# A Mamba block on one core: u = silu(conv + bias) as one Silu pass of ScalarE instead of a tanh form shared by ScalarE and VectorE

## The reference, cut to what matters

```python
xz = jnp.einsum('ed,bld->bel', in_proj_w, hidden_states)
out_f = _mamba_dir(xz, ...)
out_b = _mamba_dir(xz[:, :, ::-1], ...)[:, :, ::-1]

def _mamba_dir(xz, ...):
    x, z = xz[:, :256], xz[:, 256:]
    u = jax.nn.silu(causal_conv(x, conv_w) + conv_b)
    x_dbl = jnp.einsum('bdl,kd->bkl', u, xproj_w)            # 8 + 16 + 16 rows
    delta = softplus(einsum(dtproj_w, x_dbl[:, :8]) + dt_bias)
    dA  = exp(delta * A)                                     # 256 x 512 x 16 states
    dBx = delta * Bm * u
    h = scan(dA, dBx)                                        # along the 512 tokens
    y = einsum(h, Cm) + Dp * u
    return y * silu(z)
```

## Time and profile before

| | |
|---|---|
| device time, median of 3 runs | 922.49 us (917.73 to 923.41) |
| device time of the profiled execution | 920.03 us |
| its span, first to last instruction | 917.9 us |
| DVE busy | 814.2 us, 89% |
| ACT busy | 782.7 us, 85% |
| PE busy, POOL busy | 754.4 us, 749.2 us |
| mean granted TensorE clock | 0.942 |

### The profile page before, as it was taken

How to read it: one execution, slowest core, us unless ns; L and a number is a source line. 1 busy time by engine, 2 the same in 40 slices (tenths; PEclk the granted TensorE clock), 3 DMA queues, 4 the chain that set the end, 5 groups by cost and what they waited for, 6 DMA issues and landing times. The chain is left out here.

```text
span 917.9 us, 13850 instructions
## 1 busy us (share of the span) xinstructions
PE 754.4 (82%) x3873; PEld 377.3 (41%) x3873; DVE 814.2 (89%) x846; ACT 782.7 (85%) x1454; POOL 749.2 (82%) x446
## 2 busy tenths in 40 slices
PE   3477988889887897978898898978989787997975
PEld 1224434353443535334363535435353443634343
DVE  2249889998999989998999989999899989999995
ACT  2488998899979997999979999799979999799850
POOL 2028979889797998889798898979988897988984
PEclk9778999999999999999999999999999999999787
DMA  3242408061350707134080603407071331707000
GB/s 96 71 115 78 98 4 196 3 145 31 86 122 3 171 3 163 45 85 86 28 181 3 157 17 98 108 18 156 3 169 39 92 79 34 163 4 172 0 16 20
DMA packets 51401, 72.52 MB, mean 79 GB/s; under 512 B 6688, under 2 KB 19888, under 8 KB 51376
## 3 DMA queue, kind: packets, MB, share of 16 engines
q1 hardware_dynamic: 50944, 71.95, 33.7%
q10 hardware_dynamic: 432, 0.26, 0.1%
HBM read 60.66 MB, written 11.53 MB: 79 GB/s over the span
## 5 line engine op out<-in xcount | busy, mean ns | idle before, releaser
L693 POOL TENSOR_TENSOR hst<-hst,c_rep 128x1024 f32<-128x1024 f32 x256 | 601.3, 2372 | 113.7 <-DVE hst L580 113.6
L580 DVE TENSOR_TENSOR_SCAN hst<-da,b_ps 128x512 f32<-128x512 f32 x512 | 585.0, 1200 | 31.2 <-PE b_ps L884 12.6
L417 ACT ACTIVATE da<-rep,neg_a 128x511 f32<-128x511 f32 x512 | 337.0, 710 | 27.8 <-DVE hst L580 26.4
L884 PE MATMUL b_ps<-ident,dbx_t 128*128 128x128 f32 x1536 | 240.0, 295 | 104.3 <-DVE hst L580 100.2
L884 PEld LDWEIGHTS b_ps<-ident,dbx_t 128*128 128x128 f32 x1536 | 177.6, 148 | 247.0 <-DVE hst L580 207.3
L406 ACT ACTIVATE dbx_t<-du_t,b_t 128x256 f32<-128x256 f32 x576 | 248.3, 495 | 3.4 <-PE b_ps L884 1.9
L901 PE MATMUL y<-hst,sum_sel 128*32 128x512 f32 x1024 | 149.2, 658 | 12.8 <-POOL hst L693 12.8
L797 PE MATMUL pb<-xnt,conv_wt 128*128 128x512 f32 x256 | 120.9, 617 | 1.4 <-ACT xnt L317 0.8
L869 PE MATMUL b_ps<-t_log,spread_sel 32*128 32x512 f32 x256 | 92.7, 670 | 10.2 <-POOL t_log L749 9.0
L703 POOL TENSOR_TENSOR dbx_t<-du_t,b_t 128x1024 f32<-128x1024 f32 x48 | 91.7, 1909 | 2.7 <-ACT du_t L389 2.7
L568 DVE TENSOR_TENSOR b_ps<-b_ps,b_rep 128x1024 f32<-128x1024 f32 x64 | 77.8, 1216 | 1.6 <-PE b_ps L869 1.6
(11 more groups left out here) (111 smaller groups left out, 608.1 us busy)
## 6 DMA issues: line engine op xcount, KB each, us to landing
rep<-d_scr SPq DMA_DIRECT2D x128, 256.0 KB, 9.1
c_rep<-bc_scr SPq DMA_DIRECT2D x64, 256.0 KB, 5.1
d_scr<-t_pos SPq DMA_DIRECT2D x15, 512.0 KB, 2.9
b_rep<-bc_scr SPq DMA_DIRECT2D x64, 64.0 KB, 2.4
x_ln<-x SPq DMA_DIRECT2D x8, 256.0 KB, 3.5
x_res<-x SPq DMA_DIRECT2D x8, 256.0 KB, 2.9
out<-x_res SPq DMA_DIRECT2D x8, 256.0 KB, 6.0
conv_wt<-conv_w SPq DMA_DIRECT2D x2, 512.0 KB, 6.0
```

Source lines behind the costliest of these rows:

```text
L417: nc.scalar.activation(da[s % 2][:, j, 1:L], rep[d][h][:, j, 1:L], ACT.Exp, scale=neg_a[:, d, h, j, q:q + 1]).then_inc(decay_done, 1)
L580: nc.vector.tensor_tensor_scan(hst[s % RING][:, j, :], da[s % 2][:, j, :], b_ps[:, j, :], 0.0, ALU.mult, ALU.add).then_inc(scan_done, 1)
L693: nc.gpsimd.tensor_tensor(hst[s % RING][:, two, :], hst[s % RING][:, two, :], c_rep[d][:, q:q + 1, :].broadcast_to([P, 2, L]), ALU.mult).t ...
L884: ins = tr(b_ps[:, j, P * c:P * (c + 1)], dbx_t[(NX * d + q - 1) % 2][:, c, NJ * h + j, :, :].rearrange("p r e -> p (r e)"), ident[:, :])
```

## The change

Both ACT passes and the DVE operation on each half of u become one ACTIVATE, Silu with the convolution's bias, from the bank straight into `u[d]`. Both halves stand together in slot 1 of ACT's list, after `inputs_t(d, U, 1, 3)`. At half 0 it takes over DVE's wait for the reader of the old u (`sum_done`) and waits for `du_ready` of the unit before. The semaphores `u_step` and `u_sig`, the tile `half_bias` and the waits for `u_ready` at the softplus go; `softplus_in` takes over the wait for `delta_ready`, that of `t_exp`'s last reader. In the start-up the same two calls stand where the tanh passes stood.

```diff
-            def u_sigmoid(d, V, h):
+            def make_u(d, V, h):
                 act.wait_ge(conv_filled, 2 * V + h + 1)
-                wait(act, delta_ready, V)
-                nc.scalar.activation(t_exp[:, h, :], pb[:, 1 - h, :], ACT.Tanh, bias=half_bias[:, d, h:h + 1], scale=0.5).then_inc(u_step, 1)
-                act.wait_ge(u_step, 2 * V + h + 1)
-                nc.scalar.activation(t_exp[:, h, :], t_exp[:, h, :], ACT.Copy, bias=0.5, scale=0.5).then_inc(u_sig, 1)
+                if h == 0:
+                    wait(act, sum_done, SLOTS * (V - 2) + SKIP_AT)
+                    wait(act, du_ready, V - 1)
+                nc.scalar.activation(u[d][:, h, :], pb[:, 1 - h, :], ACT.Silu, bias=col[:, d, 0, h:h + 1]).then_inc(u_ready, 1)
...
             def softplus_in(d, V):
-                wait(act, u_ready, 2 * V + 2)
+                wait(act, delta_ready, V)
...
-            act.wait_ge(weights_ready, 3)
-            u_sigmoid(0, 0, 0)
-            u_sigmoid(0, 0, 1)
+            make_u(0, 0, 0)
+            make_u(0, 0, 1)
...
                     if s == 0:
-                        if nxt:
-                            u_sigmoid(e, V, 0)
                         if d == 1 or not first(b):
                             keep_dut(d, U, 1)
                     if s == 1:
                         inputs_t(d, U, 1, 3)
                         if nxt:
-                            u_sigmoid(e, V, 1)
+                            make_u(e, V, 0)
+                            make_u(e, V, 1)
...
-            def make_u(d, V, h):
-                dve.wait_ge(u_sig, 2 * V + h + 1)
-                wait(dve, sum_done, SLOTS * (V - 2) + SKIP_AT)
-                nc.vector.scalar_tensor_tensor(u[d][:, h, :], pb[:, 1 - h, :], col[:, d, 0, h:h + 1], t_exp[:, h, :], ALU.add, ALU.mult).then_inc(u_ready, 1)
...
-                    if s == 0 and nxt:
-                        if d == 0 and first(b):
-                            make_u(e, V, 0)
-                        make_u(e, V, 1)
...
-                    if s == 7 and not last(b):
-                        make_u(d, U + 2, 0)
```

More of the change, by code:

```diff
@@ L50, in build @@
         col = sb("col", [P, 2, 3, NH])
-        half_bias = sb("half_bias", [P, 2, NH])
         xproj = [sb(f"xproj{d}", [P, NH, 2, XC]) for d in range(2)]
@@ L137, in build @@
         conv_filled = sem("conv_filled")
-        u_step = sem("u_step")
-        u_sig = sem("u_sig")
         u_ready = sem("u_ready")
@@ L355, in first_softplus @@
             def first_softplus():
-                act.wait_ge(u_ready, 2)
                 act.wait_ge(dt_filled, 1)
@@ L599, in _ @@
             dve.wait_ge(w_loaded, DMA * W_LOADS)
-            nc.vector.tensor_scalar(half_bias[:, :, :], col[:, :, 0, :], 0.5, None, ALU.mult).then_inc(weights_ready, 1)
             for d in range(2):
@@ L618, in _ @@
             nc.vector.tensor_scalar(neg_a[:, :, :, :, :], neg_a[:, :, :, :, :], -1.0, None, ALU.mult).then_inc(weights_ready, 1)
-            make_u(0, 0, 0)
-            make_u(0, 0, 1)
             dve.wait_ge(fwt_filled, 1)
@@ L914, in _ @@
             pe.wait_ge(w_loaded, DMA * W_LOADS)
-            pe.wait_ge(weights_ready, 5)
+            pe.wait_ge(weights_ready, 4)
             x_proj(0, 0)
```

## The result

The changed kernel takes 960.7 us (median of 4 runs, 959.57 to 961.75) against 922.4 us: the ratio is 1.0427, with a 95% interval of 1.0395 to 1.0458. It is slower, as forecast, by 38.3 us instead of 24, and it lies 1.7 us above the range. The kernel before comes out mostly near 917.5 or near 922.3 us from one execution to the next, so a difference of two distances from it is open by some 4 us.

A forecast was written before the change was run, and what follows sets the result against it. ScalarE's chain to Ln was taken as the bound in backward units, nearly so in forward ones. 7 x 1.85 + 6 x 1.1 + 2.7 + 2.1 = 24.4 us on 922.5 gives 946.9, stated as 946; bounds 936 to 952, wider range 930 to 959.

The forecast's parts named there:

- where the path is: ScalarE's chain from slot 0's decays to slot 3's Ln: the path in backward units, 0.54 us from it in forward ones.
- the idle time ahead of log1p: VectorE's wait for Ln: from 7.5 us to some 45, about 4 per backward and 2.5 per forward unit.
- the loads: ScalarE, around the two Silus: Silu not in Exp's table, two loads per unit at 1.4 us each, 2.8 us.
- VectorE's saving: Two operations on u fewer, 1.3 us per unit; of no use in backward units, since VectorE waits at log1p.
- the wait for PE's steps: ScalarE, ahead of Abs: shrinks and gives back about 0.15 us in backward and 0.3 in forward units.
- the seven backward units: Units with d = 1, V = 2 to 14: Ln and log1p 1.85 us later each, 12.95 us in all.
- the six forward ones: Steady units with d = 0, V = 3 to 13: 1.1 us longer each, 6.6 us in all.
- the cover in the backward unit: The 1.22 us wait for z_proj takes up ScalarE's 0.5 us lateness; if it fails, 0.5 us are added seven times.
- rival 3: Switches cost more than their row shows, or lateness carries into the next unit: 957; chance 0.15 together with rival 4.
- signs of being wrong: No new loads, idle time ahead of log1p under 2 us a unit, or Silu with surroundings over 4.3 us a unit.
- The start-up: Before the first unit: about 1.4 us leaves the path and a 1.4 us load joins it, zero in sum.
- the first unit: V = 1: ScalarE has no wait to give back, so 2.7 us longer.

The follow-up runs named there:

- run 2: Changed kernel with three extra 128x512 matmuls on PE, filling its wait for x_dbl ahead of the steps: 942.52 us, ratio 1.0258 to the kernel before.
- run 1: Changed kernel with Tanh in place of Silu, a function that needs no new table load (u differs from the reference): 904.05 us, ratio 0.9834 to the kernel before.
- run 5: Changed kernel with Tanh for Silu and a plain Copy of a scratch tile in place of each load: 954.82 us, ratio 1.0378 to the kernel before.
- run 6: Changed kernel with a spare VectorE operation on scratch data in the two old places of the operation on u: 962.39 us, ratio 1.0458.
- run 8: Kernel before with both sigmoid halves in slot 1, VectorE's operations in slot 0, and one 128-row PE matmul behind x_proj: 929.19 us, ratio 1.0109.
- run 4: Kernel before with both sigmoid halves in ScalarE's slot 1 and both VectorE operations in slot 0, without Silu: 934.44 us, ratio 1.0167.

## Why the prediction was wrong

**Right: where the path is.** The chain from u to the Ln of slot 3, and the wait that takes the place of the one removed, are as described; the idle time ahead of log1p is 40.5 us where "some 45" was forecast. The split was less good: 3.0 us in forward and 2.4 in backward units, forecast 2.5 and 4, because in backward units part of VectorE's wait now stands ahead of the scans of slot 2, 3.11 us at 352.16 for PE's transposes. PE comes to them late behind its slow steps: in run 2 this wait is 0.59 us.

**Right: the loads.** No row showed Silu's table. The 32 new loads and run 1 settle that it is not Exp's. A load with its lost overlap costs 1.4 us (3.89 us for two loads and two Silus, 3.91 with plain passes in their place in run 5). The Trainium skill (ScalarE: Activation LUTs, "What ACT_TABLE_LOAD costs") gives 2.66 us with the drain. The trace does not agree: Silu starts at 337.97, 1.31 us behind the end of the pass ahead of the load.

**Right: VectorE's saving is of next to no use** (run 6), and Silu costs a Tanh.

**Wrong: what the late `xdbl` does on PE.** The step that failed is the one on the wait for PE's steps, which "gives back about 0.15" in backward and "about 0.3" in forward units. It gave nothing back, it grew. Before it was 0.25 us in the backward unit and 0.53 in the forward one, in ScalarE's timeline:

```profile
335.75 0.69 ACT L352 ACTIVATE t_exp<-pb,col 128x512 f32<-128x512 f32 x1 [0.25 <-PE pb L816]
...
389.13 0.69 ACT L352 ACTIVATE t_exp<-pb,col 128x512 f32<-128x512 f32 x1 [0.53 <-PE pb L816]
```

After it is 1.02 and 0.36 in the backward unit and 1.02 in the forward one. I took PE's steps as 1.98 us wherever they stand, and did not ask what PE does in the time that ScalarE comes later. It idles for 3 us, its granted clock falls to the lower level, and the steps take up to 3.78 us. From the log1p ahead, the forward unit's decays of slot 1 and its `xdbl` are late by 2.27 and 2.29 us (forecast 2.24), and its Ln by 2.56, not 1.6. In the backward unit the lateness grows from 2.6 us at `xdbl` (forecast 2.0) to 3.8 at Ln (forecast 1.85). Over the whole trace the seven backward units became 24.4 us longer for 12.95, the six forward ones 11.3 for 6.6, and the last one 3.4 for 2.1. Taking the fall away (run 2) gives 14 to 18 us back, and both units then come out at the forecast distances to within 0.3 us.

**Wrong: the cover in the backward unit.** The wait for z_proj ahead of the gate was to absorb ScalarE's lateness of 0.5 us. It stayed 1.22 us long, and the gate came 0.9 us late, counted from the log1p ahead. In run 2 it shrank to 0.98, and the gate was on time. In the changed kernel PE idles 4.93 us around that log1p and then works without a pause from 304.37 until z_proj starts at 313.29, at the lower clock for most of it. The windows of after, and one of before at the same distance from log1p:

```profile
303.60:307.10 3.50, 2.73 (x12) 1.63 (x16) 3.50 (x4) 3.50 (x9) 1.60 (x1) 0.50 0.00 0
307.10:310.10 3.00, 3.00 (x16) 1.72 (x9) 3.00 (x4) 3.00 (x7) 2.02 (x2) 0.50 0.78 250
```

```profile
294.50:298.00 3.50, 2.31 (x16) 0.99 (x16) 3.50 (x4) 3.50 (x9) 1.64 (x1) 1.00 0.00 0
```

So the lower clock, behind the longer idle time at log1p, makes z_proj late here too. That is read from the traces; nothing was run for it by itself.

**Missing among the rivals:** rival 3 named a time of 957, near what came, and that is luck: it asked for a dearer load, which did not come, or for lateness carried over, which did (the cover), but as the smaller part. The price of a slower PE was not among them, nor in the range. None of the signs of being wrong that the prediction names came either: the loads are there, log1p waits over 2 us a unit, and the passes of u take 3.89 us, under 4.3. The start-up was also not zero: the first scan came 3.2 us sooner, at 50.98 for 54.15, and the first unit became 4.0 us longer for 2.7. Behind the last log1p 1.2 us were added, where the sum had nothing.

**The place.** I did not price it apart. Run 8 shows that in the tanh form moving both halves to slot 1 costs 9 to 10 us of itself, and run 1 that one pass in the new place without loads is 14 us better than before.

## What to carry to other kernels

Before a function is exchanged for a single pass, find out which table it is in: here the two loads cost 2.8 us per unit and the passes saved are worth 1.35 us of ScalarE. A load costs nothing where it lies in idle time: the one ahead of the first Silu, at 16.23, was over at 17.51, and Silu waited for PE until 21.88. Whether Silu pays next to a switch that is there anyway was not tried. When a step on one engine comes later, look at what its successor on PE does while it waits, and price the successor at the lower clock as well: here that was over a third of the loss. A saving on an engine that waits a few microseconds further down its list was worth next to nothing here.

## What the runs showed of the hardware

The steps' four matmuls ran at the upper level of 2.4 GHz in 1.98 us and at 1.2 GHz in 3.78 us. The clock fell after waits of 3 us in nearly all units, after waits of 2 us in some, and in run 4 after only 0.57 us of idle time and four 32-row copies, but not after 0.52 us in the next unit; a single 128-row matmul in that place kept it up in every unit. What exactly decides is not settled by these runs. Useless matmuls in a free bank made the changed kernel 14 to 18 us faster.

VectorE's spare operation with all operands in SBUF took 724 to 7508 ns, median 1051, where the one on u that read a bank took 734; the cause was not looked into.
